# Slot stage of a decoder kernel: raw scores and column sums, routing half on GpSimd, attention ahead of the other lane's GRU

## What is computed

```python
Pn = rmsnorm(P, input_norm_w)                  # P: context, 77 rows per batch
k_proj = Pn @ Wk.T; v_proj = Pn @ Wv.T
for _ in range(3):
    sn = rmsnorm(slots, slot_norm_w)
    scores = einsum('bkd,bmd->bkm', sn @ Wq.T, k_proj) * SCALE
    attn = softmax(scores, axis=-2)            # over the 128 slots
    attn = attn / (attn.sum(-1, keepdims=True) + EPS)
    slots = gru_cell(einsum('bkm,bmd->bkd', attn, v_proj), slots, ...)
x = layernorm(x + slots)
route = sigmoid(x @ Wr + br)                   # 8 experts, the highest wins
```

## Time and profile before

| | us |
|---|---|
| median of 3 runs | 1859.66 (1858.59 to 1863.29) |
| profiled execution, whole time | 1859.5 |
| its span in the trace | 1857.8 |
| slot stage, beats | about 990 to 1640 |
| TensorE busy over the span | 1524.3 (82%) |
| VectorE, ScalarE, GpSimd busy | 1345.8, 1056.0, 1097.1 |

### The profile page before, as it was taken

How to read it: one execution, slowest core, us unless ns; L and a number is a source line. 1 busy time by engine, 2 the same in 40 slices (tenths; PEclk the granted TensorE clock), 3 DMA queues, 4 the chain that set the end, 5 groups by cost and what they waited for, 6 DMA issues and landing times. The chain is left out here.

```text
span 1857.8 us, 24612 instructions
## 1 busy us (share of the span) xinstructions
PE 1524.3 (82%) x6146; PEld 918.3 (49%) x6146; DVE 1345.8 (72%) x2482; ACT 1056.0 (57%) x2119; POOL 1097.1 (59%) x649
## 2 busy tenths in 40 slices
PE   4898888988888988888848888888888888847994
PEld 1343333333333333333315666666666666636994
DVE  2999989999899898999923556656565656653552
ACT  3777767767677776777624544444444444312553
POOL 1899988989999898999931112231313232141666
PEclk8899989999999998999878999999899999867997
DMA  4444444444444444444342211202020200006772
GB/s 143 136 166 152 157 160 142 167 145 152 160 154 144 166 160 148 149 154 160 125 156 81 97 40 69 102 16 96 17 96 16 96 12 8 5 24 167 207 209 63
DMA packets 105883, 214.42 MB, mean 115 GB/s; under 512 B 12162, under 2 KB 56709, under 8 KB 105744
## 3 DMA queue, kind: packets, MB, share of 16 engines
q1 hardware_dynamic: 101200, 204.50, 33.5%
q0 software_dynamic: 4544, 8.47, 1.3%
HBM read 168.28 MB, written 45.56 MB: 115 GB/s over the span
## 5 line engine op out<-in xcount | busy, mean ns | idle before, releaser
L324 POOL TENSOR_TENSOR hc<-state,c_rows 128x1024 f32<-128x1024 f32 x256 | 599.5, 2360 | 64.9 <-DVE state L506 60.5
L506 DVE TENSOR_TENSOR_SCAN state<-ps_da,inp 128x512 f32<-128x512 f32 x512 | 591.0, 1202 | 0.0
L609 PE MATMUL ps_y<-hc,ident 128*128 128x512 f32 x1024 | 509.2, 640 | 99.5 <-POOL hc L324 99.5
L398 ACT ACTIVATE ps_da<-dt,a_neg 128x512 f32<-128x512 f32 x512 | 347.7, 687 | 170.9 <-DVE state L506 157.0
L609 PEld LDWEIGHTS ps_y<-hc,ident 128*128 128x128 f32 x1024 | 202.9, 203 | 387.8 <-issue 237.8
L495 DVE TENSOR_TENSOR inp<-dtx,ps_b 128x1024 f32<-128x1024 f32 x192 | 231.4, 1205 | 55.2 <-ACT ps_b L404 37.9
L917 POOL TENSOR_TENSOR rs<-ms,m_half 128x4 f32<-128x4 f32 x48 | 54.1, 1126 | 301.7 <-DVE ms L1099 301.7
L555 PE MATMUL ps_misc<-x1T,w_conv 128*128 (+4 forms) x256 | 126.2, 640 | 37.9 <-ACT x1T L349 29.5
L311 POOL TENSOR_TENSOR inp<-dtx,b_rows 128x1024 f32<-128x1024 f32 x64 | 150.9, 2357 | 0.0
L404 ACT COPY ps_b<-b_rows 128x512 f32<-128x512 f32 x192 | 111.4, 580 | 36.0 <-issue 17.3
L1026 ACT ACTIVATE tr<-ps_r,bias 128x512 f32<-128x512 f32 x48 | 33.0, 687 | 149.2 <-PE ps_r L1385 149.2
(11 more groups left out here) (207 smaller groups left out, 2720.2 us busy)
## 6 DMA issues: line engine op xcount, KB each, us to landing
b_rows<-bc_rows SPq DMA_DIRECT2D x128, 512.0 KB, 4.7
c_rows<-bc_rows SPq DMA_DIRECT2D x128, 512.0 KB, 3.9
sorted_x<-pad_rows SPq DMA_DIRECT2D x8, 4160.0 KB, 13.3
w<-in_L_ffn_W SPq DMA_DIRECT2D x78, 256.0 KB
xrow<-sorted_x SPq DMA_DIRECT2D x39, 130.0 KB
x_tok<-in_x SPq DMA_DIRECT2D x16, 256.0 KB, 4.0
ctx<-in_ctx SPq DMA_DIRECT2D x16, 154.0 KB
out_x<-orow,target POOLq DMA_INDIRECT x78
```

Of the source, the lines that this page charges most:

```text
L324: pool.tensor_tensor(hc[:, n % RING], state[:, n % RING], over_c(c_rows[:, slot, n % 2]), ALU.mult).then_inc(hc_ready, 1)
L398: act.activation(ps_da[u % DA_RING][:], dt[:, par, c], ACT.Exp, scale=a_neg[:, c, n:n + 1]).then_inc(da_ready, 1)
L506: dve.tensor_tensor_scan(state[:, n % RING, c], ps_da[u % DA_RING][:], inp[:, n % RING, c], 0.0, ALU.mult, ALU.add).then_inc(state_ready, 1)
L609: ins = pe.matmul(ps_y[:, c], ident[:], hc[:, n % RING, c], start=False, stop=n == NS - 1)
```

## The change

- Scores are made from the raw `h` at the end of the beat before, and ScalarE copies them out of PSUM (`sc`). The root is applied afterwards: VectorE multiplies `sc` by the spread roots. `sn` is gone.
- `ssq` and `den` multiply by one column instead of 128. The division by 128 is in `mean_one`, and the eps of the denominator in an extra row of `ex` and `rse`; `dn` is gone. `ssq` and `rbc` now use bank `ps_hn`.
- `ssq`, `scores` and `ms` of the next beat stand at the end of a beat.
- VectorE does `mx` and `nmx` of one lane ahead of `pre`, `df`, `zd`, `h` of the other.
- The three products of `gates_h` are split: `hn` and `r` ahead of `den`, `z` behind it, and the second slot of `U` pieces now stands between `den` and `z`.
- Residual, root of the variance, normed rows, logits, labels and the cast of the destination move to GpSimd. The counts are made in `ps_xn` by three matmuls (`count`) and read from there.
- `sum_ctx` and `load_h` on ScalarE stand behind the new copy `sc`; at the stage's start the second load of contexts is queued ahead of the page clearing.

In the order excerpts a row is line, operation, output <- inputs, shape, and xN for N in a row. TensorE, round 0, the sixth beat, before: from `r` over `den` and `dbc` to the next `ssq`.

The diff, cut to its core:

```diff
-    PE1 = ["ssq", "rbc", "scores", "den", "dbc"]
+    PE1 = ["ssq", "scores", "rbc", "den", "dbc"]
...
-    U_PLACE = {(0, 0): ["tp0"], (0, 1): ["P0"], (1, 0): ["K0"], (1, 1): ["tp1"],
-               (2, 0): ["v00", "v01"], (2, 1): ["v02", "v03"], (3, 0): ["P1"], (3, 1): ["K1"],
-               (4, 0): ["ct0", "v10"], (4, 1): ["v11"], (5, 0): ["ct1"], (5, 1): ["v12", "v13"]}
+    U_PLACE = {(0, 0): ["P0"], (0, 1): ["tp0"], (1, 0): ["K0"], (1, 1): ["tp1"],
+               (2, 0): ["v00"], (2, 1): ["v01"], (3, 0): ["v02"], (3, 1): ["v03", "P1"],
+               (4, 0): ["K1"], (4, 1): ["v10", "v11"], (5, 0): ["v12"], (5, 1): ["v13"]}
...
             for beat, (a, it, j, q, _), (b, it2, j2, q2, par2) in beats(i, par):       # ScalarE
                 working = not (first and beat == 0)
-                attention_sq(a, it, j, q, par)
                 if working:
-                    gru_r(b, it2)
-                    gru_nz(b, it2)
+                    gru(b, it2)
...
+                attention_exp(a, it)
                 for name in u_names(beat, 0, first, last):
                     read_u(i, par, name)
-                attention_exp(a, it)
+                after_this = following(beat, i, par, last)
+                if after_this is not None:
+                    attention_sq(*after_this)
                 gru_h(a, it)
                 for name in u_names(beat, 1, first, last):
                     read_u(i, par, name)
-                if beat == 2 and not last:
+                if after_this is not None:
+                    attention_scores(*after_this[:2])
+                if beat == 1 and not last:
                     sum_ctx(i + 1, 1, (i + 1, 0))
...
-                if beat == 5 and not last and not (isinstance(i, int) and i == NQ - 2):
+                if beat == 4 and not last and not (isinstance(i, int) and i == NQ - 2):
                     sum_ctx(i + 2, 0, (i + 1, 1))
...
+        def maxima(lane, it):                                                           # VectorE
+            dve.wait_ge(scored[lane], it + 1)
             dve.wait_ge(pe1[lane], ev(PE1, "rbc", it))
-            dve.tensor_tensor(sn[lane][:], h[par][lane][:], ps_s[lane][:], ALU.mult).then_inc(dve1[lane], 1)
+            dve.tensor_tensor(sc[lane][:], sc[lane][:], ps_hn[0:M], ALU.mult).then_inc(dve1[lane], 1)
...
             for b in range(GB):                                                         # TensorE, ssq
-                ins = pe.matmul(ps_s[lane][:, b * P:(b + 1) * P], sq[lane][:, b * P:(b + 1) * P], ones[:], start=True, stop=True)
+                ins = pe.matmul(ps_hn[:, b:b + 1], sq[lane][:, b * P:(b + 1) * P], mean_one[:], start=True, stop=True)
...
-                ins = pe.matmul(ps_s[lane][:, b * P:(b + 1) * P], ex[lane][:, b * P:(b + 1) * P], rse[lane][:, b:b + 1].broadcast_to([M, P]), start=True, stop=True)
+                ins = pe.matmul(ps_s[lane][:, b:b + 1], ex[lane][:, b * P:(b + 1) * P], rse[lane][:, b:b + 1], start=True, stop=True)
...
                 if working:
                     gate_x(b, it2, par2, "r")
-                    gate_x(b, it2, par2, "xn")
                 root_spread(a, it)
                 if working:
+                    gate_x(b, it2, par2, "xn")
                     gate_x(b, it2, par2, "z")
-                scores(a, it, par)
+                if beat in (4, 5) and not first:
+                    count(beat - 4, i - 1, b, it2)
                 for name in u_names(beat, 0, first, last):
                     make_u(i, par, name, first, last)
-                gates_h(a, it, j, q, par)
+                gate_h(a, it, par, "hn", other, it2)
+                gate_h(a, it, par, "r", other, it2)
+                den(a, it)
                 for name in u_names(beat, 1, first, last):
                     make_u(i, par, name, first, last)
-                den(a, it)
+                gate_h(a, it, par, "z", other, it2)
                 den_spread(a, it)
+                after_this = following(beat, i, par, last)
+                if after_this is not None:
...
+                    ssq(c, it3, a, it)
+                    scores(c, it3, par3)
```

More of the change, by code:

```diff
@@ L720, in slot_stage @@
     hot = [sb(f"hot{k}", [P, NE, GB]) for k in range(2)]
-    counts = [sb(f"counts{k}", [P, 2, NE, GB]) for k in range(2)]
     upto = [sb(f"upto{k}", [P, NE, GB]) for k in range(2)]
@@ L727, in slot_stage @@
     mv2 = [sb(f"mv2_{k}", [P, GB, 2]) for k in range(2)]
-    veps2 = [sb(f"veps2_{k}", [P, GB]) for k in range(2)]
     rstd2 = [sb(f"rstd2_{k}", [P, GB]) for k in range(2)]
@@ L766, in back_to_bank @@
         return 1 + [any(b in banks(name) for b in banks(u)) for u in reversed(earlier)].index(True)
[L767 to L768 removed]
+    POSTV = ["stats", "aggr", "top", "less", "cand", "which", "hot", "upto", "based", "base", "chosen", "dest_f"]
+    POSTP = ["res2", "veps", "rstd", "rows", "scaled", "logits", "gate", "id", "next_id", "dest"]
     loaded = sem("slot_w_loaded")
@@ L841, in beats, with following @@
                 yield beat, att, (1, i * ITERS - 1, ITERS - 1, i - 1, 1 - par)
+    def following(beat, i, par, last):
+        if beat == 2 * ITERS - 1:
+            return None if last else (0, i * ITERS + ITERS, 0, i + 1, 1 - par)
+        lane, j = (beat + 1) % 2, (beat + 1) // 2
+        return (lane, i * ITERS + j, j, i, par)
     block = nc.Block()
@@ L1390, in _ @@
             make_u(-1, 1, name, True, False)
+        ssq(0, 0, None, 0)
         pe.wait_ge(u_read, len(CONTEXT))
+        scores(0, 0, 0)
         def body(i, par, first, last):
```

351 lines of the change are left out of this document (173 added, 178 removed).

## The result

The changed kernel took 1949.45 us (median of 4 runs, 1942.71 to 1954.93), the kernel before 1859.12 (4 runs, 1858.36 to 1863.29): a ratio of 1.0478, with a 95% interval of 1.0454 to 1.0501. The direction is that of the forecast and the time is inside its range. The size is not: +90 us where +31 was forecast, nearly the time of the rival in which the clock stays down longer (1957).

A forecast was written before the change was run, and what follows sets the result against it. Bound: a chain of waits around four engines, not one engine's load. From 1859.5, 18 for an earlier last `at` and 3 for the tail gave 1838; clock falls added 52: 1890, range 1833 to 1958 (own case 1868 to 1925).

The forecast's parts named there:

- the rival in which the clock stays down longer: One-column `ssq` and `den` might prolong low clock stretches: twice the loss, 119 us, time 1957; chance 0.18.
- Start: Stage start: first `mx` at 982.3 instead of 994.63, about 12 us earlier.
- Chain at full clock: Beat's path from `dbc` to the next: `den` at D + 10.2, 12.0 us plus second slot; D is `dbc`'s first transpose.
- ScalarE: Context sums and loads of `h` behind `sc` delay `tr` by up to 1.8 us; 22 us in all.
- GpSimd: Work moved to GpSimd: fullest list 8.3 us in beat 5, root due about D + 16, so no cost.
- this rival: In between: GpSimd's list late in beat 5 (6 x 3 us), or falls in a third of beats; 1856 to 1860, chance 0.08.
- Counts: Counts and first-slot pieces lie ahead of `den` on TensorE while it waits anyway: no cost.
- Clock: TensorE idles 2.0 us before `den`; a 3.40 us low stretch follows in 42 of 47 beats: 67 less 15, net +52.
- full-clock sum: All beats without clock falls: 631 us, from 47 x 12.0, second slots 40, ScalarE 22, loop's edge 4.
- its own sign: Main step is wrong if passes of `scores` and `r` on TensorE keep 0.12 us each in most beats.
- Tail: From the last `at` to the first late scatter: 3 us less, between -5 and +3.
- The first rival: The clock stays up, since the 2.0 us pause may be shorter or broken up: time 1838; chance 0.27.

The follow-up runs named there:

- e9: The changed kernel with two thrown-away products ahead of `den` in every beat and the counts moved behind gate `r`: 1866.61 us.
- e6: e5 with ScalarE's context sums and load of `h` moved ahead of the copy of the scores: 1848.44 us.
- e5: e3 with the second slot ahead of gate `z` and the counts of beats 4 and 5 behind that slot: 1881.55 us.
- e1: The changed kernel plus two thrown-away products ahead of `den` in beats 0 to 3 (all six in the first round): 1885.92 us.
- e4: The changed kernel with `ssq` and `den` back at 128 columns a block, nothing moved: 1926.35 us.
- e8: e6 with `ssq` and `den` back at 128 columns: 1803.88 us, ratio 0.9690 to the kernel before.
- e3: The changed kernel with gate `z` and second slot ahead of `den`, ScalarE reading the first slot ahead of the exponentials: 1859.25 us, one run.

## Why the prediction came out as it did

Against the profiled span of 1940.8 (forecast 1890 less the 1.7 outside the span, 1888.3) the miss is 52.5 us; the profiled execution was the fastest of four, and against the median the miss is 59. The direction was right; the loss came out three times as large as forecast. By the terms:

- **Start: right.** First `mx` at 979.45, forecast 982.3: -2.9.
- **Chain at full clock: right.** `den` at D + 10.24 for 10.2, a beat with a `v` piece 12.70 for 12.65. By e9, 1.1 us a round too short: some +9. One-column passes cost what eight full ones cost in time, as taken.
- **ScalarE: right, as far as shown.** `tr` is late by 1.7 in a beat with both; e6 against e5 gives 20.5 us by the spans and 33 by the medians, for the 20 of the sums.
- **GpSimd: right, with a wrong bound.** Four normed rows take 3.33 us, more than twice what I took from the earlier trace rows, but TensorE waited at most 0.74 for a root, 7.0 us in 14 waits. No sign of this rival:

```profile
1488.00 3.33 POOL L944 TENSOR_SCALAR row<-tok,mv,rstd 128x128 f32<-128x128 f32 x4 [0.38 <-POOL rstd L940]
```

- **Counts: nothing in time, but not nothing.** "First-slot pieces and the counts lie in front of `den` in time when TensorE waits anyway: nothing." At full clock `den` stood where it was summed, with waits of 0.70 and 1.13 us ahead of the counts. But the pause of up to 2.8 us (25.1 in all) now lies ahead of the counts instead of `den`, and in five beats a fall follows it with the slot, `hn` and `r` still to do: 1.66 us each where it was read, some 8 in all. They are part of the next term. The 20 us between e1 and e9 are of the same kind: e1 had 11 such falls.
- **Clock: the failed step.** The pauses came, as long as forecast (2.36 and 3.50 for 2.0 and 3), and the clock fell behind them; that part of the mechanism was right. What failed is the size, "A low stretch of 3.40 costs there half its length, 1.7 [...] Counting 42 of 47 beats: 67", net +52: there were 36 low stretches, not 42, with a mean of 238 / 36 = 6.6 us, not 3.4. Of the beats' 101.8 us over the full-clock sum (last `at` less first `mx`, 738.0, for 5.2 + 631 = 636.2) the chain takes 9, which leaves some 93 for the clock, 41 more than the prediction had.

  The place was off too: by its own sign `scores` and `r` should have been slow in most beats, and they were in 10 and 11. The common stretch of 3.4 us covers `den`, the slot and `z`; it is the long ones that reach `scores`, `r` and the next beat. (The 6.9 us that the prediction gives for the work behind the wait adds up to 6.2 by its own terms; nothing hangs on it.) Part of the excess is the one-column passes, 16 to 23 us by e4; the rest is there with 128 columns too, and its cause stays open. Those passes were the prediction's rival, and it should have had more weight, since they are the one kind of work of which no row showed the clock.

  The length could have been read before the change as well: the 0.95 in the earlier trace rows was taken for "about 19" stretches of 3.4, and the trace before has 13 of 5.0 in the mean, two of them of 10.2 like this one:

```profile
1598.50:1608.70 10.20, 10.20 (x45) 9.47 (x44) 6.87 (x19) 2.38 (x5) 1.01 (x1) 0.50 0.00 0
```

- **Tail: wrong by 5.** 1940.8 - 1717.44 = 223.4 us behind the last `at`, 221.0 before; forecast 3 less, not 2 more.

Together -2.9 + 9 + 41 + 5.4 = 52.5. The 9 is worked out from one round of e9 and the 41 is what it leaves, so the split between chain and clock is an estimate, good to some 5 us. That the time landed inside the stated range is no merit of the sum: the range was wide enough to hold the rival of 1957, which had a chance of 0.18, and the measured time lies next to it.

The first rival, that the clock stays up, was wrong in most beats. The Trainium skill ("TensorE: Matmul & The Clock Gate", section "HAM oscillation — how this bites in real kernels") warns of longer gaps than these; here a pause of 2.30 us with no work, and in e6 pauses of 1.00 and 0.34, came before a fall, so the measurement decides. The Trainium skill's next section there, "A second HAM failure mode: psum-queue depth-cycling", tells of a bf16 kernel whose frequent short idles between groups of matmuls made the clock go up and down. These traces have falls behind short idles too (0.27 us in e6 at 1149), in float32 and in another setting.

Open: why the low stretches last 3.4 us in one beat and 17 in another; which part of the low time after a fall is due to the 77-row products `scores`, `r`, `xn` and `z`, and which to the one-column passes. No run changed the former alone. Of the other parts of the change (routing on GpSimd, raw scores) none was undone alone; e8 shows that with another order and 128 columns they go with a kernel that is 3.1% faster than before.

## What to carry to other kernels

When a pause of the busiest engine moves to the head of its critical work, price not only the wait but the low clock behind it, with the length that such stretches have in a run of the new order and not in the old one; and fill it first with real work that waits for nothing (e3 and e6), since even thrown-away products gave back 63 us of 90. Read the length from the whole trace, not from one or two stretches. Look at what is queued behind every matmul that waits: an instruction that shares a bank with a late reader belongs behind all that doesn't. A matmul cut to one column saves no time when its weight loads remain, and may cost some through the clock.
